# One chain of small norm steps per batch from batch 1 on, in place of one per half batch

## The chip, the cores and the metric

The kernel runs on one core of a Trainium2 chip. The metric is the device time of one execution in microseconds, as the median of several runs.

## The reference

Four sequences of 1024 rows with 256 columns. Layer norm, a linear attention without softmax (it folds into a 256 x 256 matrix per sequence), a residual, and again layer norm followed by a transformer block with its own rms norms: grouped attention with 16 heads on 4 key heads, rotary positions and a causal softmax, and a mixture of 8 experts of which each row takes 2.

```python
x = L0_attn_x                                           # (4, 1024, 256)
x = x + attn(layernorm(x), W_theta, W_phi, W_g)         # att = (theta x)(phi x)^T / 16, no softmax
x = x + block(layernorm(x), ln1_w, ln2_w, wqkv, wo, gate_w, w13, w2)
# block: h = rmsnorm(x); q, k, v = split(h @ wqkv.T); rope; causal softmax; x += attn @ wo.T
#        h = rmsnorm(x); top 2 of 8 experts per row; out = sum_e w_e * (silu(h w1_e) * (h w3_e)) w2_e
```

Both layer norms need, for every row, the inverse root of the variance, and the rms norm behind the second is folded into the same steps. Those are the small norm steps of this text.

## The kernel before

A batch is one sequence: 8 tiles of 128 rows (TPB = 8), in two halves of 4 (HALF). A batch is first projected: `load_x`, then for each tile the statistics `stats` and `aggr` on VectorE (L1860, L1865); then `norm1`, the scale and shift of the first norm; `xn`, the normalized tile, on ScalarE (L1329); `xnT` (L2060) and `gram` (L2067) on TensorE, `square` (L2080), `x1` (L2089, added on VectorE at L1873), the statistics `stats2` and `aggr2` of the new rows (L1878, L1883), `norm2`, then `h` on ScalarE (L1336), `hT` (L2096), the projections to q and k (L2122) and `v` (L2107). For the keys and queries `split` parts each number into three bf16 parts, on ScalarE and, from batch 1 on, GpSimd (L1238 to L1245). Batches 1 to 3 are projected while the attention of batch 0 runs.

The attention goes by heads: `max` makes scores only for their row maximum (L2136 to L2144), which VectorE reduces (L1932, L1934), `maxT` turns them, `score` makes the scores again (L2156) with the maximum taken off, ScalarE takes the exponentials (L1411), GpSimd masks (L1251) and `pv` multiplies with the values (L2170). After a batch's attention come the routing of its rows and their scatter by expert. The experts (`up` at L2203 and L2218, `down` at L2240) take the last 390 us and fill gaps of TensorE before. Their weights `w13` and `w2` are loaded by SyncE (L1166, L1172) into memory that the projection used; `projected()` (L1059) holds the loads until the projection of all four batches, `v` among it, is done. TensorE runs warm-up matmuls on an identity (L2048) where the planner sees it idle.

**norm1** (L1498) is a chain of NORM1_STEPS = 13 VectorE instructions for each half batch: add epsilon, an inverse square root of 11 steps (L1478: a shift, a first guess, and three rounds at L1489, L1492 and L1495), and the shift. **norm2** (L1512) is one of NORM2_STEPS = 16, for each half batch as well, on two quantities at once, so twice as wide. Each instruction needs the one before it, and waits for it by a semaphore (`in_chain`). `go_on` (L1830) issues a chain one instruction at a time, so that others can stand between them.

**What sets the order.** `plan()` (L303) simulates the engines greedily with costs from `work_of` (a norm step: 0.08 us) and writes each engine's list of instructions, which is then fixed: an engine works its list in order. A step may be taken when all that `needs` names is done; of the ready ones the engine takes that with the earliest due time, and where none is ready, the one that is first. Due times count the `pv` steps: a batch's attention is 48 units. `project(b)` (L517) lists the steps of a batch's projection, and `spread_over` gives them due times at equal distances between the two ends in PROJECT_DUE, which are -900 and -800 for batch 0, -2 and 24, 8 and 36, 20 and 48 for batches 1 to 3. The table NUDGE (L253) adds to the due times of single stages of single batches. `per_batch` (L619) holds a stage of batch b back until all of the earlier batches' steps of it have been placed. The planner's memory of PSUM banks, its guess of each engine's clock and its warm-up matmuls follow from the same lists.

Of the kernel before, what the change touches and what calls it, by code (L numbers as in the profile page):

```python
# [17 lines left out]
P = 128  # L18
# [118 lines left out]
RSQRT_STEPS = 11  # L137
NORM1_STEPS, NORM2_STEPS, NORM3_STEPS = RSQRT_STEPS + 2, RSQRT_STEPS + 5, RSQRT_STEPS + 1

# [95 lines left out]
def adds(n):  # L235
# [20 lines left out]
        "h": {(3,): -127.4},  # L256
# [7 lines left out]
        "norm2": {(1,): -42.4},  # L264
# [38 lines left out]
def plan():  # L303
# [39 lines left out]
    def needs(step):  # L343
# [19 lines left out]
        if stage == "norm1":  # L363
            return [("aggr", b, HALF * (at[1] // NORM1_STEPS + 1) - 1)] + [(stage, b, at[1] - 1)] * (at[1] > 0)
        if stage == "xn":
            return [("norm1", b, NORM1_STEPS * (at[1] // HALF + 1) - 1)] + in_order(step) + [("hT", b - 2, TPB // 2 - 1)] * (b > 1) + [("pair",)] * (b == 1)
# [12 lines left out]
        if stage == "norm2":  # L379
            return [("aggr2", b, HALF * (at[1] // NORM2_STEPS + 1) - 1)] + [(stage, b, at[1] - 1)] * (at[1] > 0)  # L380
        if stage == "h":
            return [("norm2", b, NORM2_STEPS * (at[1] // HALF + 1) - 1)] + in_order(step)
# [6 lines left out]
        if stage == "gate_h":  # L389
            return [("v", b, 1), ("norm2", b, 2 * NORM2_STEPS - 1)] + (new_rows(b - 1) + [("gate", b - 1)] if b else [])  # L390
# [86 lines left out]
        if stage == "w13":  # L477
            i = at[0] * NE + at[1]
            return [("split_store", NBATCH - 1, QR - 1, 2)] + ([("w13", (i - 4) // NE, (i - 4) % NE)] if i > 3 else [])
        if stage == "w2":  # L480
            ready = [("split_store", NBATCH - 1, QR - 1, 2), ("x1_store", NBATCH - 1)]
            return ready + ([("w2", at[0] - 4)] if at[0] > 3 else [])
# [33 lines left out]

    def project(b):  # L517

        steps = [(0, ("load_x", b))]
        for half in range(2):  # L520
            tiles = range(half * HALF, (half + 1) * HALF)
            steps += [(half, (s, b, j)) for s in ("stats", "aggr") for j in tiles]
            steps += [(half, ("norm1", b, half * NORM1_STEPS + i)) for i in range(NORM1_STEPS)] + [(half, ("xn", b, j)) for j in tiles]
# [1761 lines left out]
```

## Time and profile before

| | us |
|---|---|
| median of 3 runs (1073.9 to 1074.64) | 1074.35 |
| the profiled execution | 1073.06 |
| its span | 1071.3 |
| TensorE busy | 1031.6 (96%) |
| VectorE busy | 759.7 (71%) |
| ScalarE busy | 581.3 (54%) |
| GpSimd busy | 417.8 (39%) |

The profiled execution is one run, 1.3 us under the median; 1.8 us of its time lie outside its span. Times in the rows are microseconds from the span's start, and those of a single instruction its duration. Durations of matmuls are modelled and overlap, so a long busy time of TensorE does not show it at its peak. PE is TensorE's matmuls, PEld its weight loads, DVE VectorE, ACT ScalarE, POOL GpSimd and SP SyncE.

### The profile page before, as it was taken

To read this page: it belongs to the slowest core of one execution; us is meant where nothing else is said; L and a number is where in the kernel's file an instruction comes from. 1 tells how busy PE (TensorE), PEld (TensorE's weight loads), DVE (VectorE), ACT (ScalarE), POOL (GpSimd) and SP (SyncE) were. 2 spreads that over 40 slices of the span, in tenths; PEclk is the share of its full clock that TensorE was granted. 3 is DMA by queue.
4 is the path that set the end of the run, shared out by engine and by line. 5 is a ranking of instruction groups with operands and counts; after the bars stand their busy time and mean duration, and the time that the engine had idled before them with its cause. 6 is when DMAs were issued, how large, how long until landed. Compare 5 with 4: busy or idle time off the path is not lost.

```text
span 1071.3 us, 19642 instructions
## 1 busy us (share of the span) xinstructions
PE 1031.6 (96%) x6546; PEld 609.5 (57%) x6546; DVE 759.7 (71%) x1811; ACT 581.3 (54%) x1124; POOL 417.8 (39%) x493
## 2 busy tenths in 40 slices
PE   7999899999999899999999999999999999999996
PEld 6766345654444333343333544456668976779995
DVE  5699988787887987899977788333494555655552
ACT  3564577547666888659665566563322344543220
POOL 2020432144743144322444514545637734443332
PEclk9999999999999999999999999999999999999999
DMA  6425122212415666644241332224344422222332
GB/s 195 125 86 156 44 71 88 71 63 69 132 57 147 205 182 202 190 116 115 83 128 64 113 104 52 66 62 90 94 89 109 91 50 45 37 40 40 51 44 23
DMA packets 85731, 101.49 MB, mean 95 GB/s; under 512 B 17632, under 2 KB 73312, under 8 KB 85632
## 3 DMA queue, kind: packets, MB, share of 16 engines
q1 hardware_dynamic: 70752, 80.60, 25.8%
q0 software_dynamic: 14880, 19.64, 9.9%
q8 instruction: 54, 0.88, 0.4%
q14 instruction: 45, 0.37, 0.1%
HBM read 55.76 MB, written 41.14 MB: 90 GB/s over the span
## 4 chain that ended last, share of the span: by engine, by line
PE 75%; DVE 16%; ACT 5%; issue 2%; DMA 1%; POOL 0%; SPq 0%; POOLq 0%; DVEq 0%; ACTq 0%
PE psum L2218 12%; PE psum L2170 10%; PE psum L2240 9%; PE psum L2156 8%; PE psum L2203 7%; DVE psum L1932 5%; PE psum L2136 5%; PE psum L2177 3%; PE psum L2212 3%; PE psum L2122 3%; PE psum L2139 2%; DVE mx L1934 2%; PE psum L2143 2%; ACT probs_mem L1411 2%; PE psum L2067 2%
## 5 line engine op out<-in xcount | busy, mean ns | idle before, releaser
L1411 ACT ACTIVATE probs_mem<-psum 128x512 f32<-128x512 f32 (+1 forms) x464 | 232.6, 594 | 82.7 <-PE psum L2156 81.9
L1932 DVE CUSTOM_DVE_ANT_1 psum<-psum,masking 128x640 f32<-128x640 f32 (+3 forms) x256 | 256.9, 1046 | 25.9 <-PE psum L2139 24.4
L1310 POOL DMA_INDIRECT out<-yout,labels x68 | 108.9, 1601 | 173.5 <-DVE yout L2012 83.5
L2156 PE MATMUL psum<-stack_mem 98*128 98x512 bf16 (+3 forms) x768 | 168.4, 328 | 7.3 <-ACT probs_mem L1411 2.9
L1251 POOL TENSOR_SCALAR_AFFINE_SELECT probs_mem<-probs_mem 128x512 f32<-128x512 f32 x104 | 68.1, 657 | 229.3 <-ACT probs_mem L1411 229.2
L1436 ACT ACTIVATE gated<-psum 128x512 f32<-128x512 f32 x68 | 40.6, 597 | 154.4 <-PE psum L2218 70.2
L2156 PEld LDWEIGHTS psum<-stack_mem 98*128 98x128 bf16 x768 | 65.5, 98 | 102.6 <-ACT probs_mem L1411 23.5
L2170 PE MATMUL psum<-probs_mem,v 128*17 128x512 f32 (+3 forms) x1152 | 117.2, 491 | 0.7 <-ACT heads_out L1418 0.5
L2240 PE MATMUL psum<-w_mem,gated 128*128 x480 | 114.5, 382 | 0.1
L1934 DVE TENSOR_REDUCE mx<-psum 128x4 f32<-128x512 f32 (+2 forms) x96 | 95.7, 1037 | 9.2 <-PE psum L2144 6.7
L2240 PEld LDWEIGHTS psum<-w_mem,gated 128*128 128x128 f32 x480 | 88.0, 190 | 23.8 <-issue 13.7
L2136 PE MATMUL psum<-stack_mem 96*128 96x512 bf16 x256 | 95.0, 385 | 3.7 <-DVE mx L1932 2.0
L2203 PE MATMUL psum<-w_mem,blockT 128*128 x200 | 94.9, 597 | 2.1 <-issue 1.4
L1411 ACT ACTIVATE gated<-psum 128x512 f32<-128x512 f32 x144 | 79.6, 622 | 26.9 <-PE psum L2156 26.6
L2002 DVE SCALAR_TENSOR_TENSOR gated<-gated,psum 128x512 f32<-128x512 f32 x68 | 46.5, 684 | 48.3 <-ACT gated L1436 48.3
L2139 PE MATMUL psum<-stack_mem 96*128 96x128 bf16 (+3 forms) x256 | 76.6, 299 | 0.0
L2006 DVE TENSOR_TENSOR gated<-psum,gated 128x512 f32<-128x512 f32 x68 | 46.9, 690 | 40.4 <-PE psum L2218 19.6
L1281 POOL DMA_INDIRECT routed<-hrow,route_mem x64 | 63.3, 989 | 20.4 <-issue 13.3
L2218 PE MATMUL psum<-blockT,probs_mem 128*128 128x128 f32 x576 | 70.2, 275 | 0.0
L1996 DVE COPY blockT<-psum 128x256 f32<-128x256 f32 x68 | 28.6, 421 | 57.4 <-PE psum L2190 57.4
L2218 PEld LDWEIGHTS psum<-blockT,probs_mem 128*128 128x128 f32 x576 | 68.6, 192 | 0.9
L2136 PEld LDWEIGHTS psum<-stack_mem 96*128 96x128 bf16 x256 | 24.8, 97 | 77.3 <-DVE mx L1932 37.6
(243 smaller groups left out, 1779.8 us busy)
## 6 DMA issues: line engine op xcount, KB each, us to landing
block<-routed SPq DMA_DIRECT2D x68, 129.0 KB, 2.2
w_mem<-in_w13T SPq DMA_DIRECT2D x16, 512.0 KB, 5.6
qk_parts<-w_mem SPq DMA_DIRECT2D x16, 384.0 KB, 2.6
stack_mem<-qk_parts SPq DMA_DIRECT2D x32, 192.0 KB, 3.2
w_mem<-in_x SPq DMA_DIRECT2D x8, 512.0 KB, 5.6
out<-w_mem SPq DMA_DIRECT2D x8, 512.0 KB, 3.7
x_late<-out SPq DMA_DIRECT2D x8, 512.0 KB, 4.9
stack_mem<-qk_parts SPq DMA_DIRECT2D x32, 128.0 KB, 2.8
```

The lines of the kernel that those rows point to most:

```text
L1251: e.affine_select(pb[:, :, q0:q0 + P], pb[:, :, q0:q0 + P], [[0, GRP], [1, P]], ALU.is_ge, 0.0, base=0, channel_multiplier=-1).then_inc(se ...
L1310: e.indirect_dma_start(out_rows, bass.IndirectOffsetOnAxis(ap=to, axis=0), youts[w % NYOUT], None, bounds_check=NBATCH * SEQ - 1, oob_is_e ...
L1411: e.activation(probs[probs_of(m)][:, hh:hh + n, q0:CH], grid(turn[step][0][:, 0:n * (CH - q0)], n), ACT.Exp, scale=float(HD) ** -0.5).then ...
L1932: e.tensor_tensor_reduce(keys, keys, masked(w), 1.0, -3e38, ALU.add, ALU.max, to).then_inc(sem["max"], 1)
L1934: e.tensor_reduce(to, took, AX.X, ALU.max).then_inc(sem["max"], 1)
L2136: e.matmul(bk[:, 0:CH], rows_of, s[0:STACK, 0, GRP, :], start=True, stop=True)
L2139: m = e.matmul(to, rows_of, s[0:STACK, r, GRP, 0:w], start=True, stop=True)
L2156: m = e.matmul(bk[:, i * (CH - q0):(i + 1) * (CH - q0)], s[0:STACK + NMAX, kt // TPR, GRP, kt % TPR * P:(kt % TPR + 1) * P], s[0:STACK + N ...
L2170: m = e.matmul(pv_bank[32 * hh:32 * hh + HD + 1, q0:CH], v1[:, b, kt, g, :], pb[:, hh, q0:CH], start=(kt == KEYS[r][0]), stop=(kt == KEYS[ ...
L2203: m = e.matmul(bk, blockT[w % 2][:, k], w13_s[:, k, bass.ds(offset[w] + half * FFN, FFN)], start=(k == 0), stop=(k == KD - 1))
L2218: m = e.matmul(bk[:, c * P:(c + 1) * P], slots[copies_of(w)[0] % NSLOT][:, k, half * FFN + c * P:half * FFN + (c + 1) * P], blockT[w % 2][ ...
L2240: m = e.matmul(bk[:, 0:D], rowsT[:, k * P:(k + 1) * P], w2_mem[:, bass.ds(offset[w] + k * D, D)], start=(k == 0), stop=(k == KF - 1))
```

## The change

Batch 0 keeps its two chains. From batch 1 on `norm1` and `norm2` are one chain for all 8 tiles (`norm_parts(b)` is 1 if b is not 0, else 2), with the same number of steps and instructions of twice the width. The chain waits for the statistics of all 8 tiles, and in the planner for the end of the batch before's chain; `xn` and `h` of either half wait for the one chain. The lists in `project` follow: statistics of both halves, one chain, eight `xn`; and for the second norm all `aggr2`, one chain, then for each half its `h`, `hT` and projections. So a batch has 29 steps fewer, and the rest have other due times between the same ends. In the table, two entries change places: h of batch 3 (-127.4) and norm2 of batch 1 (-42.4) become norm2 of batch 3 (-127.4) and h of batch 1 (-42.4). In the planner `w13` and `w2` now also need the last `v`, and `w13` the last `x1_store`. The semaphore counts are adapted everywhere.

```diff
@@ -135,6 +135,16 @@
+def norm_parts(b):
+    return 1 if b else 2
+def norm_parts_before(b):
+    return sum(norm_parts(i) for i in range(b))
...
@@ -253,7 +263,7 @@
-        "h": {(3,): -127.4},
+        "h": {(1,): -42.4},
...
@@ -261,7 +271,7 @@
-        "norm2": {(1,): -42.4},
+        "norm2": {(3,): -127.4},
...
@@ -361,9 +371,9 @@
-            return [("aggr", b, HALF * (at[1] // NORM1_STEPS + 1) - 1)] + [(stage, b, at[1] - 1)] * (at[1] > 0)
+            return [("aggr", b, (TPB if b else HALF * (at[1] // NORM1_STEPS + 1)) - 1)] + [(stage, b, at[1] - 1)] * (at[1] > 0) + [(stage, b - 1, norm_parts(b - 1) * NORM1_STEPS - 1)] * (b > 0 and not at[1])
-            return [("norm1", b, NORM1_STEPS * (at[1] // HALF + 1) - 1)] + in_order(step) + [("hT", b - 2, TPB // 2 - 1)] * (b > 1) + [("pair",)] * (b == 1)
+            return [("norm1", b, (1 if b else at[1] // HALF + 1) * NORM1_STEPS - 1)] + in_order(step) + [("hT", b - 2, TPB // 2 - 1)] * (b > 1) + [("pair",)] * (b == 1)
...
@@ -377,9 +387,9 @@
-            return [("aggr2", b, HALF * (at[1] // NORM2_STEPS + 1) - 1)] + [(stage, b, at[1] - 1)] * (at[1] > 0)
+            return [("aggr2", b, (TPB if b else HALF * (at[1] // NORM2_STEPS + 1)) - 1)] + [(stage, b, at[1] - 1)] * (at[1] > 0) + [(stage, b - 1, norm_parts(b - 1) * NORM2_STEPS - 1)] * (b > 0 and not at[1])
-            return [("norm2", b, NORM2_STEPS * (at[1] // HALF + 1) - 1)] + in_order(step)
+            return [("norm2", b, (1 if b else at[1] // HALF + 1) * NORM2_STEPS - 1)] + in_order(step)
...
@@ -476,9 +486,10 @@
-            return [("split_store", NBATCH - 1, QR - 1, 2)] + ([("w13", (i - 4) // NE, (i - 4) % NE)] if i > 3 else [])
+            ready = [("split_store", NBATCH - 1, QR - 1, 2), ("x1_store", NBATCH - 1), ("v", NBATCH - 1, 1)]
+            return ready + ([("w13", (i - 4) // NE, (i - 4) % NE)] if i > 3 else [])
-            ready = [("split_store", NBATCH - 1, QR - 1, 2), ("x1_store", NBATCH - 1)]
+            ready = [("split_store", NBATCH - 1, QR - 1, 2), ("x1_store", NBATCH - 1), ("v", NBATCH - 1, 1)]
...
@@ -514,22 +525,34 @@
+    def one_part(b, half, n):
+        at = half if b == 0 else 0
+        return range(at * n, (at + 1) * n)
-            steps += [(half, ("norm1", b, half * NORM1_STEPS + i)) for i in range(NORM1_STEPS)] + [(half, ("xn", b, j)) for j in tiles]
+            if b and not half:
+                continue
+            steps += [(half, ("norm1", b, i)) for i in one_part(b, half, NORM1_STEPS)] + [(half, ("xn", b, j)) for j in (range(TPB) if b else tiles)]
-            steps += [(6 + half, ("aggr2", b, j)) for j in tiles] + [(6 + half, ("norm2", b, half * NORM2_STEPS + i)) for i in range(NORM2_STEPS)]
-            steps += [(6 + half, ("h", b, j)) for j in tiles] + [(8 + half, ("hT", b, half * HALF // 2 + c)) for c in range(HALF // 2)]
-            steps += [(8 + half, (s, b, half)) for s in ("k_mm", "q1_mm", "q2_mm")]
+            steps += [(6 + half, ("aggr2", b, j)) for j in tiles]
+            if b and not half:
+                continue
+            steps += [(6 + half, ("norm2", b, i)) for i in one_part(b, half, NORM2_STEPS)]
+            for at in range(2) if b else (half,):
+                steps += [(6 + at, ("h", b, j)) for j in range(at * HALF, (at + 1) * HALF)]
+                steps += [(8 + at, ("hT", b, at * HALF // 2 + c)) for c in range(HALF // 2)]
+                steps += [(8 + at, (s, b, at)) for s in ("k_mm", "q1_mm", "q2_mm")]
...
@@ -1498,9 +1521,10 @@
-                for half in range(2):
-                    s, m = (v[:, b % 2][:, :, half * HALF:(half + 1) * HALF] for v in (rt, mv.rearrange("p s t c -> p s c t")))
-                    q.wait_ge("aggr", TPB * b + HALF * (half + 1))
+                n = TPB // norm_parts(b)
+                for part in range(norm_parts(b)):
+                    s, m = (v[:, b % 2][:, :, part * n:(part + 1) * n] for v in (rt, mv.rearrange("p s t c -> p s c t")))
+                    q.wait_ge("aggr", TPB * b + n * (part + 1))
...
@@ -1512,10 +1536,11 @@
-                for half in range(2):
-                    s, m, scale, shift = (v[:, :, half * HALF:(half + 1) * HALF] for v in (
+                n = TPB // norm_parts(b)
+                for part in range(norm_parts(b)):
+                    s, m, scale, shift = (v[:, :, part * n:(part + 1) * n] for v in (
-                    q.wait_ge("aggr2", TPB * b + HALF * (half + 1))
+                    q.wait_ge("aggr2", TPB * b + n * (part + 1))
...
```

## Rows read from the trace of the kernel before

**Rows 1.** Page, part 1: busy us (share) xinstructions of each engine.

```profile
PE 1031.6 (96%) x6546; PEld 609.5 (57%) x6546; DVE 759.7 (71%) x1811; ACT 581.3 (54%) x1124; POOL 417.8 (39%) x493
```

**Rows 2.** Page, part 4: the chain that ended last, by engine.

```profile
PE 75%; DVE 16%; ACT 5%; issue 2%; DMA 1%; POOL 0%; SPq 0%; POOLq 0%; DVEq 0%; ACTq 0%
```

**Rows 3.** Busy us of each engine in stretches, with count, clock, DMA.

```profile
40.00:320.00 280.00, 270.90 (x1659) 145.81 (x1658) 236.65 (x572) 175.89 (x354) 99.77 (x102) 1.00 0.30 89
...
320.00:680.00 360.00, 346.61 (x2343) 144.25 (x2342) 300.89 (x704) 251.36 (x530) 130.44 (x171) 1.00 0.44 128
...
320.00:360.00 40.00, 37.08 (x251) 17.14 (x250) 33.59 (x87) 28.80 (x68) 10.27 (x17) 1.00 0.59 181
...
400.00:440.00 40.00, 39.23 (x286) 13.47 (x284) 31.94 (x61) 33.24 (x65) 16.59 (x22) 1.00 0.68 201
```

**Rows 4.** Timeline (start us, us, engine, line), VectorE and GpSimd, 62 to 74.

```profile
64.66 0.16 DVE L1489 SCALAR_TENSOR_TENSOR rt<-rt 128x4 f32<-128x4 f32 x1
64.86 0.16 DVE L1492 TENSOR_TENSOR rt<-rt 128x4 f32<-128x4 f32 x1
...
70.76 2.28 POOL L1242 TENSOR_TENSOR w_mem<-w_mem 128x512 f32<-128x512 f32 x2 [6.74 <-ACT w_mem L1401]
...
71.98 1.08 DVE L1489 SCALAR_TENSOR_TENSOR rt<-rt 128x4 f32<-128x4 f32 x1
```

**Rows 5.** Timeline, VectorE: the last norm step of batch 3.

```profile
251.70 0.17 DVE L1534 SCALAR_TENSOR_TENSOR shifts<-scales,mv 128x8 f32<-128x8 f32 x1
```

**Rows 6.** Timeline, VectorE, 19 to 31: batch 1's first chain begins.

```profile
19.97 0.15 DVE L1505 TENSOR_SCALAR rt<-mv 128x4 f32<-128x4 f32 x1
...
21.43 0.24 DVE L1865 BATCH_NORM_AGGREGATE mv<-st 128x2 f32<-128x6 f32 x2
...
30.68 0.69 DVE L1873 TENSOR_TENSOR w_mem<-psum,w_mem 128x512 f32<-128x512 f32 x1 [8.38 <-PE psum L2089]
```

**Rows 7.** Timeline, VectorE and GpSimd, 119 to 125.

```profile
119.70 2.51 POOL L1238 TENSOR_TENSOR w_mem<-w_mem 128x512 f32<-128x512 f32 x2
...
120.01 1.00 DVE L1482 TENSOR_SCALAR rt<-rt 128x4 int32<-128x4 int32 x1
```

**Rows 8.** Chain that ended last, in order: start us, us, what.

```profile
31.37 0.07 DVE rt L1489
...
38.96 0.07 DVE rt L1492
...
62.12 0.08 DVE rt L1505
...
251.70 0.18 DVE shifts L1534
```

**Rows 9.** TensorE's waits, 60 to 330 us: total, times, longest.

```profile
PE psum L2143 <- DVE mx L1934: 4.2, 2, 2.9
...
PE psum L2136 <- DVE mx L1932: 0.5, 2, 0.3
PE psum L2156 <- DVE mx L1932: 0.3, 1, 0.3
```

**Rows 10.** Timeline, TensorE: warm-ups, batch 1's gram, one wait.

```profile
36.53 3.58 PE L2048 MATMUL psum<-ident 128*128 128x128 f32 x30
...
53.47 3.62 PE L2067 MATMUL psum<-w_mem 128*128 128x256 f32 x16
...
125.89 0.39 PE L2143 MATMUL psum<-stack_mem 96*128 96x512 bf16 x1 [2.92 <-DVE mx L1934]
```

**Rows 11.** Timeline, ScalarE: the last four h of batch 3.

```profile
251.90 2.08 ACT L1336 ACTIVATE w_mem<-w_mem,shifts,scales 128x256 f32<-128x256 f32 x4 [1.55 <-DVE shifts L1534]
```

**Rows 12.** Timeline: first and last weight load, first expert matmul.

```profile
324.16 0.34 SPq L1166 DMA_DIRECT2D w_mem<-in_w13T  x1
...
456.04 0.43 SPq L1172 DMA_DIRECT2D w_mem<-in_w2T  x1
...
557.73 1.55 PE L2203 MATMUL psum<-w_mem,blockT 128*128 x3 [0.23 <-issue]
```

More of the change, by code:

```diff
@@ L389, in needs @@
         if stage == "gate_h":
-            return [("v", b, 1), ("norm2", b, 2 * NORM2_STEPS - 1)] + (new_rows(b - 1) + [("gate", b - 1)] if b else [])
+            return [("v", b, 1), ("norm2", b, norm_parts(b) * NORM2_STEPS - 1)] + (new_rows(b - 1) + [("gate", b - 1)] if b else [])
         if stage in ("k_mm", "q1_mm", "q2_mm"):
@@ L617, in plan @@
         streams.append((spread_over(at, at + 8, [("base", b, j) for j in range(TPB)]), False))
-    per_batch = {"load_x": 1, "x1_store": 1, "x1_load": 1, "stats": TPB, "aggr": TPB, "norm1": 2 * NORM1_STEPS, "xn": TPB, "xnT": TPB // 2, "gram": 0, "square": 2, "x1": TPB // 2,
-                 "stats2": TPB, "aggr2": TPB, "norm2": 2 * NORM2_STEPS, "h": TPB, "hT": TPB // 2, "v": 2, "k_mm": QR, "q1_mm": QR, "q2_mm": QR,
+    per_batch = {"load_x": 1, "x1_store": 1, "x1_load": 1, "stats": TPB, "aggr": TPB, "norm1": 0, "xn": TPB, "xnT": TPB // 2, "gram": 0, "square": 2, "x1": TPB // 2,
+                 "stats2": TPB, "aggr2": TPB, "norm2": 0, "h": TPB, "hT": TPB // 2, "v": 2, "k_mm": QR, "q1_mm": QR, "q2_mm": QR,
                  "split": 15 * QR, "split_store": 3 * QR, "xhat": TPB, "wo": TPB, "base": TPB, "square_sum": TPB, "norm3": NORM3_STEPS, "h2": TPB,
@@ L1323, in _ @@
                     b, j = at
-                    q.wait_ge("norm1", NORM1_STEPS * (2 * b + j // HALF + 1))
+                    q.wait_ge("norm1", NORM1_STEPS * (norm_parts_before(b) + (1 if b else j // HALF + 1)))
                     q.wait_ge("hT_mm", TPB // 2 * (b - 1))
@@ L1332, in _ @@
                     o = b % 2
-                    q.wait_ge("norm2", NORM2_STEPS * (2 * b + j // HALF + 1))
+                    q.wait_ge("norm2", NORM2_STEPS * (norm_parts_before(b) + (1 if b else j // HALF + 1)))
                     q.wait_ge("gram_mm", nth["gram", b, gram_steps(b) - 1])
@@ L1338, in _ @@
                     b, j = at
-                    q.wait_ge("norm2", 2 * NORM2_STEPS * (b + 1))
+                    q.wait_ge("norm2", NORM2_STEPS * norm_parts_before(b + 1))
                     q.wait_ge("x1_load", 32 * (b + 1))
@@ L1530, in norm2 @@
                     in_chain("norm2")
-                    e.tensor_tensor(ratios[:, b, half * HALF:(half + 1) * HALF], s[:, 2], s[:, 1], ALU.mult).then_inc(sem["norm2"], 1)
+                    e.tensor_tensor(ratios[:, b, part * n:(part + 1) * n], s[:, 2], s[:, 1], ALU.mult).then_inc(sem["norm2"], 1)
                     yield
                     in_chain("norm2")
-                    e.scalar_tensor_tensor(shift, scale, -1.0, m[:, 0].unsqueeze(1).broadcast_to([P, 2, HALF]), ALU.mult, ALU.mult
+                    e.scalar_tensor_tensor(shift, scale, -1.0, m[:, 0].unsqueeze(1).broadcast_to([P, 2, n]), ALU.mult, ALU.mult
                                            ).then_inc(sem["norm2"], 1)
@@ L1863, in _ @@
                     q.wait_ge("stats", nth["stats", b, j])
-                    q.wait_ge("norm2", 2 * NORM2_STEPS * (b - 1))
+                    q.wait_ge("norm2", NORM2_STEPS * norm_parts_before(b - 1))
                     e.bn_aggr(mv[:, b % 2, j], st[:, b % 2, j]).then_inc(sem["aggr"], 1)
@@ L1959, in _ @@
                     q.wait_ge("v_out", 4 * (b + 1))
-                    q.wait_ge("norm2", 2 * NORM2_STEPS * (b + 1))
+                    q.wait_ge("norm2", NORM2_STEPS * norm_parts_before(b + 1))
                     q.wait_ge("logits", b)
```

## The prediction

> **What bounds the kernel now.** I first read the busy shares: TensorE is busy 96% of the span, VectorE 71% [rows 1]. A busy TensorE row need not be TensorE at its peak, so the next view is the chain of work that ended last: TensorE holds 75% of it, VectorE 16%, ScalarE 5% [rows 2]. TensorE sets the time over most of the span, with stretches in which VectorE does. The stages say where. TensorE is idle 280 - 270.90 = 9.1 us from 40 to 320 us (the attention of batch 0, in whose gaps batches 1 to 3 are projected), 360 - 346.61 = 13.4 us from 320 to 680 us, and the other stages are outside the reach of this edit except through the order [rows 3]. VectorE is busy 236.65 of 280 us in the first of these, 85% [rows 3], the fullest it is in any long stage. All norm steps of batches 1 to 3 lie between 19.97 and 251.87 us [rows 5, 6].
>
> **What is removed.** One chain of norm1 has 13 steps, one of norm2 has 16. Batches 1 to 3 lose one of each: 3 x 29 = 87 VectorE instructions. The steps that stay are twice as wide, 128x8 for 128x4 and 128x16 for 128x8. The rows bound what that costs: a step takes 0.16 us at 128x4 and 0.17 at 128x8 [rows 4, 5], so under 0.02 us a step over 87 steps, at most 1.7 us of VectorE time; I take 1.
>
> What a removed step was worth depends on its place. In an unbroken chain each starts 0.20 us after the one before (64.66, 64.86) [rows 4]. Beside other VectorE work a step takes far less: squeezed in at the start it holds 0.07 us of the path [rows 8], so 0.08 is my low end. And some last about a microsecond: L1489 at 71.98 took 1.08 us, beside TENSOR_TENSORs of GpSimd from 70.76 to 73.04; L1482 at 120.01 took 1.00 beside GpSimd's from 119.70 to 122.21 [rows 4, 7]. So the removed time is between 87 x 0.08 = 7 and 87 x 0.24 = 21 us, the second figure being what one step holds of VectorE over the 148 steps from 62 to 252 us (35.8 us of distance to the next instruction; first and last in rows 8, 5). I take 16 us of VectorE time.
>
> The trace shows long steps beside GpSimd's two-input operation for a two-input step (L1489) and for a one-input one (L1482) alike [rows 4, 7]. The Trainium skill (GPSIMD Engine Reference, Specifications) says that GpSimd shares its SBUF interfaces with VectorE and lists contention for instructions with two SBUF inputs or in a two-port mode; by that rule alone the one-input steps might be free of it. The sum here goes by the rows either way.
>
> **How much of it is on the path.** In the chain that ended last, norm steps of batches 1 to 3 hold 6.5 us from 62 to 74 us (26 pieces), 1.5 us around 93 us (9), 4.2 us from 119 to 125 us (9) and 7.2 us from 237 to 252 us (32): 19.4 us in 76 pieces, first and last of them (62.12, 251.70) in rows 8. Halved, that is 9.7 us, an upper bound. The lower bound is what TensorE really stood still for: from 60 to 330 us it waited 4.2 us for L1934 and 0.5 + 0.3 us for L1932, the maxima on VectorE, 5.0 us in all [rows 9]. 2.92 of them are one wait, at 125.89 [rows 10], behind a run of norm1 steps of batch 3 in which three last 0.98 to 1.05 us (the first of them is in rows 7). The rest of the path's VectorE time is covered by TensorE's other matmuls, and shortening it brings those forward but removes none. I take half of the 5.0: **2.5 us**.
>
> **The startup.** Batch 1's eight statistics are ready at 21.7 us, VectorE then stands idle 8.38 us (to 30.68), with nine of the first half's 13 steps done [rows 6]; the other four and the second half's 13 come behind it. From 30.68 to 39.17 VectorE is on the path of batch 0 (x1, norm2, h), and batch 1's norm1 steps squeezed in hold about 0.9 us of it (12 pieces, first and last in rows 8). One chain of 13 started near 21.7 fits for the most part into the idle time, so **0.5 us** of that goes. What is late next: batch 1's xn. Before, gram of batch 1 came at 53.47, while TensorE ran 30 warm-up matmuls, 3.58 us, at 36.53 [rows 10]. If all eight xn follow one early chain (2.08 us for four such passes of ScalarE [rows 11], so 4.2 us in all, in the gap ahead of batch 0's h), half of gram can take the place of the warm-up matmuls, work worth 3.5 us (the 16 matmuls at 53.47 hold 3.62 [rows 10]). Bounds 0 (its order may put it behind, as before) to 3.5; I take **1.5 us**, since the order decides and not readiness.
>
> **What the change adds.** Each batch's first four xn, h, hT and k/q projections now wait for all eight statistics and for one chain. Queued behind on ScalarE: xn and h are four at a time 2.08 us; the second four of batch 3's h began at 251.90 straight after the second chain [rows 5, 11]. One chain ends about 3 us earlier than the second did, and the first four no longer run under it; the pair of halves then takes 2.1 us more of unhidden ScalarE. The cover is the distance to the attention of batch 1: its projection is due to end at 24 of the 48 units that batch 0's attention lasts, and those of batches 2 and 3 at 36 and 48. So I book 0, with 2 us for each batch where the cover fails. The added wait between one batch's chain and the next is met in any case, since the batches already follow each other.
>
> The added needs of the expert weight loads (v and x1_store of batch 3) move nothing on VectorE. Before, the last v of batch 3 was over by 306, the first load went out at 324.16 and the last at 456.04, while the first expert matmul is at 557.73 [rows 12]. With some 6 us to land, they have 95 us to spare. Cost 0; were v to slip behind about 400 us, it would tell.
>
> The moved due times (h of batch 1, norm2 of batch 3) and the smaller number of steps over which the due times are spread change the order of all engines behind the first difference. That is no cost by itself, it is the spread of the forecast.
>
> **Sum.** 2.5 + 0.5 + 1.5 = 4.5 us less. The profiled execution took 1073.06 us (span 1071.3 and 1.8 around it), 1.3 under the median 1074.35. 1073.06 - 4.5 = 1068.6, on the scale of the medians 1069.9.
>
> **The rivals.**
> 1. *The whole half of the path, and the pulled-in gram.* 9.7 + 3.5 = 13.2: 1061. For it: VectorE is the chain from 62 to 74 us almost without TensorE. Against: only 5.0 us of waits there. 10%.
> 2. *Nothing comes out.* TensorE's matmuls fill what VectorE gives back, then TensorE's total stays: within 2 us, 1074. For it: TensorE is idle in only 9.1 of 280 us [rows 3]. 20%. The Trainium skill (Perfetto Trace Analysis, Identifying the Most-Contended Engine) says to optimize the most contended engine first, and to judge TensorE by weight-load and flop use rather than by matmul busy time. By its first half this change brings nothing; by its second TensorE (57% weight-load busy) may not be as full as it looks.
> 3. *The order is dealt anew, and worse.* The order is made by a greedy planner from due times with nudges of single stages; a change in one place re-deals everything after. Place: the maxima-bound stretches from 320 to 680 us. There the loosest 40 us has 2.9 us of TensorE idle (320 to 360) and a tight one 0.8 (400 to 440) [rows 3]; if five of the nine stretches go from the tight to the loose level, 5 x 2.1 = 10.5 us come on, less the 4.5 gained: 1080. It decides from 2 to 3 such stretches on. Against: the new order may also be better. 26%.
> 4. *The chain as a block.* Norm2 of batch 3 is now 127 units early. A chain put in one piece ahead of a maximum holds TensorE as at 125.89, 2.92 us [rows 10]. With four of the six chains so: 4 x 2.9 = 11.7, less the two waits of now (4.2) and the 2.0 of the startup: +5.5, 1080. It decides from three on (+2.6). Against: a chain is 13 x 0.2 = 2.6 us, and TensorE mostly has scores at hand. 10%.
> That the change does not do what it says would show as more than 13 + 16 steps in a batch; I give it no chance worth a figure.
>
> **How the numbers follow.** Forecast (1066 to 1072) 34%, rival 1 10%, rival 2 20%, rival 3 26%, rival 4 10%. About 0.2%, 2.1 us, can be told from no change. Faster 0.34 + 0.10 = 0.44, same 0.20, slower 0.36. The range takes in rival 1 nearly whole, and most of rivals 3 and 4: 1062 to 1083.
>
> **What would show it.** 13 + 16 norm steps a batch from batch 1 on, all with 128x8 and 128x16; VectorE's busy time down by 12 to 18 us from 759.7; TensorE's waits for L1934 from 60 to 330 us under 4.2 us; fewer than 30 warm-up matmuls from 36 to 40 us, gram of batch 1 before 53 us; idle of TensorE from 320 to 680 us still about 13.4 us. The last one is where it would go wrong: if it grows beyond 18 us, rival 3 holds. If VectorE's time falls and TensorE's waits do not, rival 2 does.

## The result, and the profile after

The changed kernel takes 1083.45 us (median of 5 runs, 1081.9 to 1086.01), the kernel before 1074.64 us beside it. The ratio of the runs is 1.0076 (95% interval 1.0059 to 1.0092): 0.76% slower, 8.2 us, where 4.5 us less was forecast. Every loss or gain in us below is such a ratio times the median of the kernel before; where two of these are subtracted, both intervals count, so a difference of 5 us is known to about 2.4. The changed kernel's profiled execution, at 1081.9 us one of the two fastest of its five runs, has a span of 1080.1 us, 8.8 more than before.

The page of the changed kernel: busy time of each engine (part 1) and the chain that ended last by engine (part 4), against [rows 1] and [rows 2]. Lines of TensorE, and the maxima of VectorE, stand 25 further down than before (L1932 is now L1957, L1934 L1959, L2048 L2073, L2067 L2092), those of ScalarE and GpSimd 23.

```profile
PE 1040.0 (96%) x6600; PEld 615.9 (57%) x6600; DVE 749.4 (69%) x1724; ACT 579.0 (54%) x1124; POOL 420.5 (39%) x493
...
PE 78%; DVE 14%; ACT 4%; issue 2%; DMA 1%; POOL 1%; SPq 0%; POOLq 0%; DVEq 0%
```

VectorE has 87 instructions fewer and 10.3 us less to do. TensorE has 54 instructions *more* and is busy for 8.4 us longer (1031.6 to 1040.0), while its idle time over the span hardly moved: 1071.3 - 1031.6 = 39.7 us before, 1080.1 - 1040.0 = 40.1 after. So the loss stands in a busy row. The stretches of the changed kernel, against [rows 3] (length, then busy us and count of PE, PEld, DVE, ACT, POOL, then clock, DMA share, GB/s):

```profile
40.00:320.00 280.00, 274.23 (x1678) 146.33 (x1677) 225.69 (x500) 177.13 (x361) 100.00 (x102) 0.99 0.30 92
320.00:680.00 360.00, 344.82 (x2362) 146.06 (x2362) 301.10 (x699) 249.45 (x526) 129.79 (x169) 1.00 0.44 126
```

TensorE's idle time fell from 9.1 to 5.8 us between 40 and 320 us, as hoped, and rose from 13.4 to 15.2 us between 320 and 680 us, well under the 18 that the prediction named as the sign of rival 3. The warm-up matmuls by themselves show what TensorE's added busy time is made of. First the kernel before, then the changed one, groups by line (busy us, mean ns), then the changed one's by stretch:

```profile
L2048 PE MATMUL psum<-ident 128*128 128x128 f32 x90 | 15.1, 321 | 0.0
```

```profile
L2073 PE MATMUL psum<-ident 128*128 128x128 f32 x144 | 23.7, 306 | 0.4 <-DVE mx L1957 0.3
```

```profile
320.00:450.00 130.00, 2.37 (x14) 2.11 (x14) 0.99 0.62 182
450.00:520.00 70.00, 7.60 (x46) 6.37 (x46) 1.00 0.37 104
520.00:680.00 160.00, 0.49 (x2) 0.30 (x2) 1.00 0.32 91
```

All 54 added TensorE instructions are warm-up matmuls, 8.6 us of them; the 6456 others are busy for the same time in both kernels (1031.6 - 15.1 = 1016.5 us before, 1040.0 - 23.7 = 1016.3 after). Before, the stretch from 450 to 520 us had 6 warm-up matmuls (1.36 us), now it has 46. The planner puts them where it sees nothing else to do: they are waiting, written as work. (The Trainium skill, Perfetto Trace Analysis, Identifying the Most-Contended Engine, says that matmul busy time does not show how close TensorE is to its limit, because matmuls are pipelined, and takes weight-load busy time and flop use instead. Here too the busy row misleads, but by filler; and the filler went into the weight-load row as well, 609.5 to 615.9 us, so that row misleads with it.) The `pv` matmuls of both kernels in three stretches show what the useful work does meanwhile (busy us and count, clock, DMA share, GB/s), before, then after:

```profile
0.00:440.00 440.00, 82.58 (x816) 1.00 0.41 121
440.00:500.00 60.00, 17.20 (x168) 1.00 0.43 124
500.00:680.00 180.00, 45.76 (x456) 1.00 0.32 92
```

```profile
0.00:440.00 440.00, 84.98 (x824) 0.99 0.40 120
440.00:500.00 60.00, 14.50 (x144) 1.00 0.46 127
500.00:680.00 180.00, 48.32 (x480) 1.00 0.32 91
```

Up to 440 us the changed kernel is ahead (824 to 816). In the next 60 us it does 144 for 168. TensorE's busy time without its warm-up matmuls says how far each kernel has come: by 440 us it is 403.6 us before and 405.3 after, by 500 us 460.4 and 455.8, by 680 us 634.9 and 627.0. So the changed kernel is 1.7 us ahead at 440 us, 4.6 behind at 500 and 8.0 behind at 680. Its last norm step of batches 1 to 3 starts at 238.9 us: where norm steps run, it gains, and it loses where none of them stands any more. What runs from 440 us on is the attention of batch 2, as the timeline of the changed kernel shows (start us, us, engine, line):

```profile
480.14 0.38 PE L2164 MATMUL psum<-stack_mem 96*128 96x512 bf16 x1
...
480.36 2.47 PE L2073 MATMUL psum<-ident 128*128 128x128 f32 x18
480.59 0.14 DVE L1957 DVE_READ_ACCUMULATOR2_ANT mx<- 128x1 f32 x1
480.59 1.26 DVE L1957 CUSTOM_DVE_ANT_1 psum<-psum,masking 128x1024 f32<-128x1024 f32 x1
...
481.77 1.26 DVE L1957 CUSTOM_DVE_ANT_1 psum<-psum,masking 128x1024 f32<-128x1024 f32 x1
...
483.24 0.60 ACT L1441 ACTIVATE heads_out<-psum 128x512 f32<-128x512 f32 x1 [6.45 <-PE psum L2195]
```

VectorE reduces one maximum after another, ScalarE has stood still for 6.45 us, and TensorE multiplies an identity. Ahead of this place other work has slipped. `wo` of batch 1 (the output projection behind its attention), whose matmuls started from 451.8 to 470.5 us before, has them from 459.7 to 474.8. Followed back, each step of that slip has its instruction:

| start, us | before | after |
|---|---|---|
| rank of batch 0 (TensorE, L2184 / L2209) | 358.33 | 365.01 |
| routing weights copied into the rows (L1991 / L2016) | 373.6, 406.0 | 390.6, 423.4 |
| last scatter of batch 0's rows (L1281 / L1304) | 431.26 | 449.90 |
| `xhat` of batch 1 (L1343 / L1366) | 437.0 | 455.4 |
| `wo` of batch 1 (L2177 / L2202) | 451.8 | 459.7 |

The logits of batch 0 are there at 350 us in both. Its routing is a string of small VectorE steps with a due time put off by 108.5 units (NUDGE, `route`), so it gets only the slots that the maxima leave. The new order leaves it others, and it slides by 7 us up to its rank step and by 17 to 19 us from there on; `xhat` of batch 1, the normalized rows, needs the memory of the rows (hrow) that batch 0's scatter reads, and follows by 18 us.

### The profile page after: what moved, and what is told of

Its sections match the earlier page's. It is cut to its first block, busy times and chain, and to the rows that moved or that the text cites. A ratio compares the mean times of both kernels' runs of the same rounds, so it can differ in the third digit from the quotient of the medians.

```text
span 1080.1 us, 19663 instructions
## 1 busy us (share of the span) xinstructions
PE 1040.0 (96%) x6600; PEld 615.9 (57%) x6600; DVE 749.4 (69%) x1724; ACT 579.0 (54%) x1124; POOL 420.5 (39%) x493
## 4 chain that ended last, share of the span: by engine, by line
PE 78%; DVE 14%; ACT 4%; issue 2%; DMA 1%; POOL 1%; SPq 0%; POOLq 0%; DVEq 0%
PE psum L2243 12%; PE psum L2195 10%; PE psum L2265 9%; PE psum L2181 8%; PE psum L2228 8%; DVE psum L1957 5%; PE psum L2161 4%; PE psum L2147 4%; PE psum L2237 3%; PE psum L2202 2%; PE psum L2164 2%; DVE mx L1959 2%; ACT probs_mem L1434 2%; PE psum L2168 2%; PE psum L2092 2%
## 5 line engine op out<-in xcount | busy, mean ns | idle before, releaser
L1957 DVE CUSTOM_DVE_ANT_1 psum<-psum,masking 128x640 f32<-128x640 f32 (+3 forms) x256 | 256.0, 1047 | 28.0 <-PE psum L2164 27.2
L1959 DVE TENSOR_REDUCE mx<-psum 128x4 f32<-128x512 f32 (+2 forms) x96 | 96.1, 1038 | 12.6 <-PE psum L2169 8.1
L2265 PEld LDWEIGHTS psum<-w_mem,gated 128*128 128x128 f32 x480 | 88.2, 190 | 24.5 <-issue 14.6
L1304 POOL DMA_INDIRECT routed<-hrow,route_mem x64 | 63.7, 995 | 25.7 <-issue 13.0
L2243 PE MATMUL psum<-blockT,stack_mem 128*128 128x128 f32 x544 | 66.2, 275 | 0.0
```

The source lines that it names most:

```text
L1957: e.tensor_tensor_reduce(keys, keys, masked(w), 1.0, -3e38, ALU.add, ALU.max, to).then_inc(sem["max"], 1)
L1959: e.tensor_reduce(to, took, AX.X, ALU.max).then_inc(sem["max"], 1)
L2243: m = e.matmul(bk[:, c * P:(c + 1) * P], slots[copies_of(w)[0] % NSLOT][:, k, half * FFN + c * P:half * FFN + (c + 1) * P], blockT[w % 2][ ...
L2265: m = e.matmul(bk[:, 0:D], rowsT[:, k * P:(k + 1) * P], w2_mem[:, bass.ds(offset[w] + k * D, D)], start=(k == 0), stop=(k == KF - 1))
```

## The experiments

Twelve kernels. The ratio is against the kernel before on the same chip, with its 95% interval.

**The removed steps alone, in the old order.** The chains of the second halves of batches 1 to 3 are left out, and their four tiles take the scale and shift of the first half's, so the result is not the reference's. The order of all that is left is as before.

```diff
+                    if b and half:
+                        for _ in range(NORM1_STEPS):
+                            yield
+                        return
```

> The kernel before with its order of work untouched; the second norm1 and norm2 chain of batches 1 to 3 is left out (87 VectorE instructions), and the second four tiles take the scale and shift of the first four, so this part of the result is not the reference's. It measures what the removed steps are worth where the order stays. Theory A (the removed steps help and the new order is what costs): faster than before by 2 to 6 us, 1069 to 1073. Rival B (the steps are hidden, TensorE fills the gaps anyway): within 1 us of before. Rival C (the one chain itself costs, by its waits): says nothing here, since the first chains stay.

Measured: 1071.79 us for 1076.4, 0.9961 (0.9948 to 0.9974). That is 4.2 us less (2.8 to 5.6), 0.05 us for each of the 87 steps: theory A. VectorE is busy 222.59 us between 40 and 320 us for 236.65 [rows 3], and TensorE 273.39 for 270.90. So leaving the steps out gives about what the prediction booked for them, as long as the order does not move.

**The steps put back, in the new order.** Each norm step of batches 1 to 3 is issued once for each half, one straight after the other.

```diff
-                next(chains[make, key])
+                    chains[make, key] = [make(*key, (part,)) for part in range(2)] if both else [make(*key)]
+                for chain in chains[make, key]:
+                    next(chain)
```

> The changed kernel with its order of work untouched, but each norm step of batches 1 to 3 issued twice, once for either half and each waiting for the one before, as in the kernel before: the 87 VectorE instructions are back. Theory A: slower than the changed kernel's 1083.5 by 3 to 8 us, since 87 steps of some 0.2 us are put where a chain already stands on VectorE: 1087 to 1091. Rival B: within 1 us of 1083.5. Rival C (what costs in the changed kernel is the one chain standing as a block ahead of the maxima): doubling the block doubles that cost, 9 us more, 1092.

Measured: 1100.55 us, 1.0216 (1.0190 to 1.0242), 1.40% over the changed kernel: 15 us, 0.17 us a step, above all three forecasts. The stretch tells where:

```profile
40.00:320.00 280.00, 263.39 (x1566) 141.40 (x1566) 222.76 (x547) 166.80 (x338) 93.28 (x96) 0.98 0.29 85
```

TensorE is idle for 16.6 us there, for 5.8 in the changed kernel. This miss was the first sign that a norm step costs more in the new kernel than in the old one.

**The two table entries alone.** The kernel before, with h of batch 3 and norm2 of batch 1 out of the table, norm2 of batch 3 and h of batch 1 in it.

```diff
-        "h": {(3,): -127.4},
+        "h": {(1,): -42.4},
...
-        "norm2": {(1,): -42.4},
+        "norm2": {(3,): -127.4},
```

> The kernel before with two chains, only the two entries of the table exchanged as in the change (h of batch 3 and norm2 of batch 1 become norm2 of batch 3 and h of batch 1). The planner's own clock ends at 1061.4 us for it, at 1050.8 for the kernel before and 1061.9 for the changed one. Theory A (the order is what costs; the table was fitted to the old order and any difference loses the fit): 8 to 10 us over before, 1082 to 1085. Rival C (the one chain costs): within 2 us of before, 1073 to 1077.

Measured: 1087.55 us, 1.0109 (1.0090 to 1.0128). No step is removed and no wait is added, and 11.7 us are lost, even more than theory A's 8 to 10: an order alone can do as much as the whole change does. It isn't the same picture, though: only 8 warm-up matmuls are added (1.1 us), TensorE is idle for 47.6 us instead of 39.7, and its other matmuls are busy 5.2 us longer.

**The changed kernel with the old entries.** The same exchange, backwards.

> The changed kernel with one chain and the two entries of the table as they were in the kernel before. The planner's clock ends at 1067.3 us, 5.4 over the changed kernel's. Theory A: slower than the changed kernel by 3 to 6 us, 1086 to 1090. Rival D (the two exchanged entries are what costs, the chain is harmless): back to 1072 to 1076.

Measured: 1084.78 us, 1.0076 (1.0059 to 1.0094), the same as the changed kernel. Neither theory had this. With the new set of steps the old entries do no better than the new ones, so the loss can't be put down to these two entries alone.

**The warm-up matmuls left out.** The changed kernel without the 31 warm-up steps (62 matmuls) that its list has after some 100 us. No part of the result depends on them.

```diff
+                if stage == "warm" and at[0] >= 41:
+                    continue
```

> The changed kernel, order untouched, with the 31 warm-up steps left out that its planner places after 100 us (two matmuls each; they compute nothing). The changed kernel has 72 such steps, the kernel before 45. Theory A (the warm-up matmuls only fill time in which TensorE has nothing; the time is lost by the order): within 2 us of the changed kernel, 1082 to 1086, with TensorE's busy time down by 5 to 7 us and its idle time up by as much. Rival E (the extra warm-up matmuls themselves hold TensorE up): 4 to 6 us faster, about 1078, unless the clock falls.

Measured: 1081.82 us, 1.0068 (1.0047 to 1.0089), within the interval of the changed kernel: theory A. The matmuls are filler, and their time doesn't come back. 11.3 us of them are out; TensorE is idle for 3.6 us more (43.7 for 40.1), and the other 6456 matmuls are busy for 6.9 us more (1035.6 - 12.4 = 1023.2 for 1016.3), at a mean clock of 0.990 for 0.994.

**Batch 0's routing held back, in the kernel before.** In the planner the first routing weights may not start before 382 us, 18 us after the 364 that it gives them otherwise. Then the same with 372 us.

```diff
+            if step == ("weight", 0, 0):
+                start = max(start, 382.0)
```

> The kernel before with two chains and its table; the planner alone is told that the first weight step of batch 0 cannot start before 382 us on its clock, where it stands at 364 otherwise and at 382.5 in the changed kernel. So batch 0's rows are scattered some 20 us later and xhat of batch 1 after them. Nothing else is changed. The planner's clock then ends at 1063.4 us (1050.8 before), with 68 warm-up steps. Theory F (the changed kernel loses at the close of batch 1, because batch 0's routing slid back): 8 to 12 us slower than before, 1083 to 1087, with the same loss of TensorE's work between 440 and 500 us. Rival G (the late scatter is beside the point): within 2 us of before.

> The kernel before, with only batch 0's first routing weights held back to 372 us in the planner, 8 us later than it gives them there, where the earlier run held them back by 18 us. The planner's end is 1058.4 us, 7.6 us over its own; the earlier run's was paid in full and lost 11.8 us on the chip. Theory F (a late routing of batch 0 costs time through what queues behind it): +5 us if the loss goes by the lateness (8 of 18 us), +7.6 us if it goes by the planner's end, so 1079 to 1083 us, with the warm-up matmuls between 450 and 500 us that the kernel before doesn't have. Rival: up to some 10 us of lateness there is slack before batch 1's wo needs the buffer: 1074 to 1076 us.

Measured: 1086.41 us, 1.0109 (1.0088 to 1.0130), and 1082.47 us, 1.0072 (1.0046 to 1.0098): 11.7 and 7.7 us lost, where the planner's own end moved by 12.6 and 7.6. Theory F in both; the second loss goes by the planner's end and not by the lateness. The first one shows much of the changed kernel's picture without the change. Its `pv` matmuls, then its warm-up matmuls:

```profile
0.00:440.00 440.00, 83.37 (x816) 1.00 0.40 121
440.00:500.00 60.00, 13.91 (x144) 1.00 0.42 122
```

```profile
440.00:500.00 60.00, 6.67 (x42) 1.00 0.42 122
```

144 for 168 `pv` matmuls and 42 warm-ups for 6, as in the changed kernel (144, 46). Unlike there, TensorE is also idle for 5.7 us more than before (45.4 for 39.7). The second one has 152 `pv` matmuls and 22 warm-ups in this stretch.

**Batch 0's routing brought forward, in the changed kernel.** The late due time of `route` goes, `rank` gets an early one.

```diff
-        "route": {(0,): 108.5, (2,): -8},
+        "rank": {(0,): -50.0, (2,): 14.4},
+        "route": {(2,): -8},
```

> The changed kernel with two entries of the table altered: batch 0's routing without its delay of 108.5 units, and its rank step 50 units early. The planner's clock ends at 1053.7 us (1061.9 in the changed kernel), with 51 warm-up steps, and batch 0's last row is sent at 435 instead of 448 on that clock. Theory F: 6 to 9 us faster than the changed kernel, 1075 to 1078. Rival G: within 2 us of the changed kernel, 1082 to 1086.

Measured: 1077.11 us, 1.0030 (1.0014 to 1.0046). 0.46% or 4.9 us come back, under theory F's 6 to 9 by the ratios, though the median lies in its 1075 to 1078. The warm-up matmuls from 440 to 500 us are 6 again:

```profile
440.00:500.00 60.00, 1.36 (x6) 0.97 0.42 116
```

3.2 us to the kernel before remain. How late batch 0's routing ran on the chip in these kernels, and how much each lost (starts in us; first copy of the routing weights, `xhat` and `wo` of batch 1):

| kernel | weights | xhat | wo | lost |
|---|---|---|---|---|
| before | 373.6 | 437.0 | 451.8 | |
| changed | 390.6 | 455.4 | 459.7 | 8.2 |
| before, routing to 382 | 392.6 | 456.8 | 461.6 | 11.7 |
| before, routing to 372 | 384.1 | 447.9 | 453.2 | 7.7 |
| changed, routing early | 379.0 | 441.6 | 454.8 | 3.2 |
| new entries alone | 382.4 | 446.3 | 452.1 | 11.7 |
| changed, old entries | 398.9 | 459.7 | 464.1 | 8.2 |

So the slid routing is a cause: put into the old order it costs time, and drawn back in the new one it gives time back. It is not the measure of the loss. Each of these edits re-deals the order behind it as well, the two entries lose 11.7 us with a routing 9 us late and the old entries 8.2 with one 25 us late, and no run brought the routing all the way back to where it was. What it is worth is therefore known only as the 4.9 us that came back.

**Shorter chains in the new order.**

```diff
-                    yield from rsqrt("norm1", s[:, 0], s[:, 1], s[:, 2], s[:, 3])
+                    yield from rsqrt("norm1", s[:, 0], s[:, 1], s[:, 2], s[:, 3], 1 if b else 3)
```

> The changed kernel's order, with two of the three Newton rounds left out of the inverse square roots of the norms of batches 1 to 3: 36 of the chains' VectorE steps are not issued. Theory P (in this order each step of a chain stands on the path, at the price that issuing 87 more of them had: 17.1 us over 87 is 0.20 us each): 7 us less, 1075.5 to 1077.5 us. Rival H (the steps hide in gaps between maxima, and the doubled chain was dear only because it outgrew the gaps that the order leaves for it): 1081.5 to 1084 us, as the changed kernel.

Measured: 1077.06 us, 1.0018 (1.0005 to 1.0030), 0.58% or 6.2 us under the changed kernel: 36 steps at 0.17 us, the price that putting 87 back had. Theory P. (With fewer rounds the inverse roots are less exact, so this is no version to use.) The time comes in while norm steps run: without warm-up matmuls TensorE is 5.4 us ahead of the kernel before by 440 us (the changed kernel 1.7). From 440 to 500 us it then falls back by 6.2 us, as the changed kernel does by 6.3. TensorE is busy 277.23 of the 280 us from 40 to 320:

```profile
40.00:320.00 280.00, 277.23 (x1704) 148.91 (x1704) 220.26 (x473) 180.36 (x369) 101.35 (x104) 1.00 0.30 92
```

**One batch alone.** One chain for batch 2, two for batches 1 and 3 (`return 1 if b == 2 else 2` in `norm_parts`, and the lists by it), with the changed table.

> The changed kernel with its table, but one chain in place of two for batch 2 alone: batches 1 and 3 keep a chain for each half, so 29 VectorE steps are gone where the change removes 87. The planner's end is 1052.0 us with 45 warm-up steps, beside 1050.8 with 45 for the kernel before. Theory O (removed steps help, and what loses is the order that a particular table and set of steps happen to give): the removed steps of batch 2 are worth about a third of the 4.2 us measured for all three batches at the old order, so 1073.5 to 1076.5 us, no slower than the kernel before, with about 15 us of warm-up matmuls. Rival W (whole-batch norms themselves delay the xn and h of the first half, and so the following stages): a third of the changed kernel's loss or more, 1077 to 1080 us.

Measured: 1075.79 us for 1074.37, 1.0017 (1.0003 to 1.0030). No gain was left of the 1.4 us that a third of the removed steps would give. The median lies in theory O's range and under rival W's; but the loss of 1.8 us (0.3 to 3.2) lies between O's "no slower" and W's third of 2.7 us and shuts out neither.

**A table searched for the changed kernel.** Due times were changed at random and the table with the earliest end on the planner's clock was kept: one with 21 entries changed, and one after a longer search.

> The changed kernel with 21 entries of the table of due times replaced or added, an early state of the search whose end ran at 1082.7 us. The planner's end is 1049.1 us with 41 warm-up steps, 12.8 us under the changed kernel's and 1.7 under the kernel before's. Theory M (the planner judges moderate changes of the table rightly, and the long search found states that are good on its clock alone): as the runs that lie 21.5 to 24 us above the planner's end, 1070.5 to 1073 us, with a granted clock of 0.993 or more. Rival V (any search on the planner's clock buys its gain by leaving TensorE without filler where the chip then waits): as the searched run, 36 us above, 1082 to 1086 us, with TensorE idle over 18 us between 320 and 680 us and a clock at or under 0.988.

> The changed kernel with its chains as they are and a table of due times searched anew for them (the table is input of the planner alone; the program computes the same). The planner's own end is 1046.5 us on its clock with 40 warm-up steps, against 1050.8 with 45 for the kernel before and 1061.9 with 72 for the changed one. Theory O (the changed kernel lost by its order, and the order is judged rightly by the planner): the runs so far lie 21.5 to 24 us above the planner's end, so 1068 to 1071 us, with warm-up matmuls back from 23.7 us to at most 15 us and VectorE's busy time at 749 us. Rival: the loss lies in the chains themselves, or a table fitted to the planner's clock fits nothing on the chip: 1075 us or more.

Measured: 1084.87 us, 1.0085 (1.0058 to 1.0111), and 1082.72 us, 1.0066 (1.0050 to 1.0082). The rivals hold (in the profiled run with 21 entries TensorE is idle for 21.3 us between 320 and 680 us, as rival V has it, at a mean clock of 0.989, just over its 0.988). On the planner's clock these tables beat both kernels; on the chip they are no better than the changed kernel. All kernels whose order differs, together (the planner's end, the median, the first taken from the second, and of the profiled run the busy time of warm-up matmuls and TensorE's idle time over the span):

| kernel | planner's end | median | difference | warm-ups, us | TensorE idle, us |
|---|---|---|---|---|---|
| before | 1050.8 | 1074.64 | 23.8 | 15.1 | 39.7 |
| changed | 1061.9 | 1083.45 | 21.6 | 23.7 | 40.1 |
| new entries alone | 1061.4 | 1087.55 | 26.2 | 16.2 | 47.6 |
| changed, old entries | 1067.3 | 1084.78 | 17.5 | 23.5 | 42.6 |
| before, routing to 382 | 1063.4 | 1086.41 | 23.0 | 21.3 | 45.4 |
| before, routing to 372 | 1058.4 | 1082.47 | 24.1 | 17.5 | 45.1 |
| changed, routing early | 1053.7 | 1077.11 | 23.4 | 16.7 | 39.7 |
| batch 2 alone | 1052.0 | 1075.79 | 23.8 | 14.0 | 40.1 |
| changed, 21 entries | 1049.1 | 1084.87 | 35.8 | 13.1 | 45.7 |
| changed, long search | 1046.5 | 1082.72 | 36.2 | 13.1 | 45.7 |

The planner's end plus 24 gives seven of the eight kernels above within 2.4 us and the eighth within 6.5, and misses the two searched ones by 12. Their profiled runs say where the time is: against the kernel before, TensorE is idle for 6.0 us more in both, the 6456 matmuls that aren't warm-ups are busy for 6.7 us (21 entries) and 9.4 us (long search) more, at mean clocks of 0.989 and 0.985 for 0.996, and 2.0 us of warm-up matmuls are gone. So of the 10.7 and 13.4 us by which their spans are longer, over half is matmuls that last longer. (The profiled run of the long search is the slowest of its six.) Its trace shows one place where both come about. Stretches of 3.4 us (PE busy, clock, DMA share, GB/s), and TensorE's and GpSimd's lines of the timeline:

```profile
446.80:450.20 3.40, 3.20 (x19) 1.00 1.07 371
...
453.60:457.00 3.40, 2.42 (x6) 0.74 1.07 235
457.00:460.40 3.40, 0.49 (x1) 0.50 0.31 103
460.40:463.80 3.40, 3.40 (x18) 0.50 0.15 52
463.80:467.20 3.40, 3.40 (x20) 0.75 0.13 41
```

```profile
457.43 2.34 POOL L1297 TENSOR_TENSOR attnT<-attnT,recip_rows 128x1024 f32<-128x1024 f32 x1 [7.62 <-DMA recip_rows<-recips]
...
459.91 2.10 PE L2211 MATMUL psum<-wo_s,attnT 128*128 128x264 f32 x4 [2.95 <-POOL attnT L1297]
```

The weight loads and the reading back of the softmax's reciprocals (recip_rows) fall into one stretch there. The DMA share is 1.07, GpSimd waits 7.62 us for that transfer and TensorE 2.95 us for GpSimd, and no warm-up matmul stands there, because on the planner's clock nothing waits. This is one such place, read from the trace; that such places make up the whole 12 us is not shown.

## Why the prediction was wrong

**The removed steps: right in size at the old order, partly by luck.** They were put at 2.5 + 0.5 + 1.5 us; leaving them out with the order kept gave 4.2 us (2.8 to 5.6). The sum fits, but not by its parts: 1.5 us of it is a pulled-in gram, which can't come in that experiment, so the 4.2 stand against 3.0.

**VectorE's time: too high in the new order alone.** 16 us were taken, with 12 to 18 as the sign; 10.3 came, 0.12 us a step. With the order kept the same 87 steps were worth 14.6 us (759.7 to 745.1), 0.17 us a step. The sum had it right, and the new order took 4.3 of it back: in batch 3's chain of norm1, from 116.26 to 126.21 us, six of the 13 steps last 0.55 to 1.19 us, with TENSOR_TENSORs of GpSimd running from 116.61, 120.09, 123.11 and 124.83; and one product with `ratios` (L1990) lasts 2.73 us, where the four of the kernel before (L1965) last 0.21 to 0.23.

**The path between 60 and 330 us: right in size.** Of the 4.2 us of waits for L1934 (now L1959) 0.6 are left; TensorE's waits of the changed kernel in that stretch, for [rows 9]:

```profile
PE psum L2168 <- DVE w_mem L1898: 2.1, 1, 2.1
PE psum L2181 <- DVE w_mem L1932: 0.6, 1, 0.6
PE psum L2174 <- DVE mx L1959: 0.6, 1, 0.6
PE psum L2161 <- DVE mx L1957: 0.6, 2, 0.3
```

A new one of 2.1 us, for x1, has come. Over 40 to 320 us 3.3 us of idle time are gone.

**The startup and the gram: wrong, 2.0 us.** The signs were fewer than 30 warm-up matmuls and a gram before 53 us. The first came by two matmuls, the second didn't:

```profile
36.24 3.29 PE L2073 MATMUL psum<-ident 128*128 128x128 f32 x28
...
54.84 3.40 PE L2092 MATMUL psum<-w_mem 128*128 128x256 f32 x15
```

The gram came 1.4 us later than [rows 10], and the idle time of VectorE is still there:

```profile
22.07 0.17 DVE L1529 TENSOR_SCALAR rt<-mv 128x8 f32<-128x8 f32 x1
...
23.08 0.17 DVE L1518 SCALAR_TENSOR_TENSOR rt<-rt 128x8 f32<-128x8 f32 x1
...
31.27 0.69 DVE L1898 TENSOR_TENSOR w_mem<-psum,w_mem 128x512 f32<-128x512 f32 x1 [8.02 <-PE psum L2114]
31.87 0.16 DVE L1512 SCALAR_TENSOR_TENSOR rt<-rt 128x8 f32<-128x8 f32 x1
```

Six of the 13 steps are over at 23.25, then the order has batch 0's x1 next. The chain was ready for it; the list was not. The prediction gave this as the lower bound ("the order decides and not readiness") and took a value above it all the same.

**Wider steps, added waits and needs.** A step of 128x8 with nothing beside it lasts 0.17 us, as put (the rows above). The wait of the first halves for the whole batch's chain, booked at 0, has no cost that shows where it stands: by 440 us the changed kernel is 1.7 us ahead. The new needs of `w13` and `w2` change nothing in the plan of either kernel.

**The step that failed: "That is no cost by itself, it is the spread of the forecast."** The re-dealt order was booked at 0, with a rival of 26% on its bad side. The measured difference to the forecast is 8.2 + 4.5 = 12.7 us. The removed steps by themselves gave 4.2 us, near their 4.5, so 12.4 us stand against whatever else the change brings, and the runs point at the order: nothing is lost up to 440 us, all of it behind the last norm step; two table entries lose 11.7 us with no step removed; a late routing put into the old order loses 7.7 and 11.7 us; and 4.9 us came back with two entries for batch 0's routing. It was no even spread to begin with: taking any single entry out of the old table leaves the planner's end where it is (within 0.01 us) or makes it later, in 93 cases out of 93, by 8.5 us in the median. On its own clock the table is at an optimum for its set of steps, and from there a re-deal leads down. The planner, which needs no chip, ends at 1050.8 us for the kernel before and at 1061.9 for the changed one. That warning of 11.1 us could be had before the forecast, and the prediction doesn't use it.

**Rival 3: right in cause and nearly in size, wrong in its sign.** It was to cost 10.5 us between 320 and 680 us, in five loose stretches, and to show as idle time of TensorE beyond 18 us. The loss does lie there: 1.7 us ahead at 440 us became 4.6 behind at 500 and 8.0 behind at 680. But it shows as warm-up matmuls, mostly from 460 to 500 us, and idle time is 15.2 us. By the sign that the prediction set, rival 3 would have been struck out while being true.

**Rival 4, the chain as a block,** was put at 10% and may have something of the truth: a norm step is worth 0.05 us in the kernel before (87 left out) and 0.17 us in the changed one (36 left out, 87 put back), where the prediction had one price. These aren't the same steps. Before, whole second chains went; in the changed kernel the steps belong to the one chain on which both halves wait. Whether the order or the longer chain makes them dearer is open, since no run shortened the chains in the old order. It does not show as the single long waits that the rival named.

**What stays open.** Of the 12.7 us, the slid routing accounts for at least the 4.9 that came back. For the rest, 7.8 us, no single string was found. That it belongs to the order too is likely, for the kernel before loses as much by two table entries, but it is not shown: the share of the dearer steps wasn't measured by itself, and the run with batch 2 alone doesn't shut out that whole-batch chains delay the stages behind them. No version was found that beats the kernel before with correct norms; the nearest are batch 2 alone (1.0017) and the early routing (1.0030).

## What to carry to other kernels

Where a planner writes the order from hand-fitted due times, the first price of an edit is that of a re-dealt order, and after a fit it is a loss in expectation. Run the planner on both versions before you forecast. Keep the order and leave out the work alone to see what the edit is worth, then fit the table again, with the chip and not the planner as the judge. Take filler instructions (warm-up matmuls here) out before comparing busy times. What a small step costs depends on where it stands: 0.05 us in one of these kernels, 0.17 in the other.

## What the runs showed of the hardware

A wait of TensorE can cost more than its length. In the kernel of the long search TensorE had waited 0.73 and 0.58 us (453.97 and 455.15) when the granted clock fell from 1.00 to 0.50, from 2.4 to 1.2 GHz; then came the wait of 2.95 us, and after it TensorE was busy for all of 3.40 us at 0.50 and for the next 3.40 at 0.75 (rows above). With no warm-up matmul after 100 us the mean clock of this kernel is 0.985, for 0.996 before and 0.994 changed: 1084.7 x (1 - 0.985) = 16.3 us of full clock are missing, 1071.3 x (1 - 0.996) = 4.3 before, and its 6456 other matmuls are busy for 9.4 us more. Leaving the filler out of the changed kernel (0.98 for 1.00 between 320 and 680 us) made them busy for 6.9 us more too, yet cost nothing that could be measured: they stretched into the time that the filler had held. Which of the two it will be, no run here tells beforehand.

A transfer needed soon can land late beside ones that aren't needed yet. In the same kernel, with the DMA share at 1.07, GpSimd waited 7.62 us for recip_rows<-recips, issued from 444.11 on, beside weight loads of 512 KB each (the last three ahead of it issued from 442.14 on) for experts whose first matmul runs at 573.5 us.
